# Reordering the last eight heads of the first tile in a cross-attention kernel, with eight halved slots instead of fourteen

## What is computed

```python
q = (tgt @ Wq.T).reshape(B, N, NH, dk).transpose(0, 2, 1, 3)
k = (memory @ Wk.T).reshape(B, N, NH, dk).transpose(0, 2, 1, 3)
v = (memory @ Wv.T).reshape(B, N, NH, dk).transpose(0, 2, 1, 3)
scores = jnp.einsum('bhqd,bhkd->bhqk', q, k) * scale
probs = jax.nn.softmax(scores, axis=-1)
att = jnp.einsum('bhqk,bhkd->bhqd', probs, v)
att = att.transpose(0, 2, 1, 3).reshape(B, N, D)
tgt2 = att[0]
return tgt + tgt2
```

## Time and profile before

| | before |
|---|---|
| median of 3 runs | 188.64 us (187.71 to 188.74) |
| profiled execution, its time | 188.64 us |
| its span | 186.6 us |
| busy: PE, DVE, ACT, POOL | 130.9, 102.1, 96.8, 78.1 us |
| DMA: bytes, mean rate | 71.52 MB, 383 GB/s |
| DMA packets, under 2 KB | 31424, 9008 |
| granted clock of PE, mean over the span | 0.894 |

### The profile page before, as it was taken

How to read it: one execution, slowest core, us unless ns; L and a number is a source line. 1 busy time by engine, 2 the same in 40 slices (tenths; PEclk the granted TensorE clock), 3 DMA queues, 4 the chain that set the end, 5 groups by cost and what they waited for, 6 DMA issues and landing times.

```text
span 186.6 us, 3336 instructions
## 1 busy us (share of the span) xinstructions
PE 130.9 (70%) x1224; PEld 91.9 (49%) x1224; DVE 102.1 (55%) x163; ACT 96.8 (52%) x225; POOL 78.1 (42%) x43
## 2 busy tenths in 40 slices
PE   6999999999996887998978998889885000000000
PEld 6978857677654555556756556656553000000000
DVE  0263226625527989857399659665353999900000
ACT  2344536378266979877789669798892000000000
POOL 1000000000006989800049999079992999800000
PEclk9999999999999999999999999999999755555555
DMA  6999999999999989989999999999999999999995
GB/s 218 356 357 420 407 410 412 408 409 407 411 410 384 329 297 343 341 291 319 401 386 396 393 404 407 406 404 407 411 421 413 403 416 419 407 423 421 421 420 223
DMA packets 31424, 71.52 MB, mean 383 GB/s; under 512 B 1840, under 2 KB 9008, under 8 KB 31280
## 3 DMA queue, kind: packets, MB, share of 16 engines
q1 hardware_dynamic: 31408, 71.31, 99.6%
HBM read 37.75 MB, written 33.55 MB: 382 GB/s over the span
## 4 chain that ended last, share of the span: by engine, by line
PE 54%; ACT 15%; DVE 11%; issue 6%; DVEq 1%; POOL 0%; ACTq 0%; POOLq 0%
PE bank L410 12%; PE bank L390 8%; ACT probs L609 8%; PE bank L350 8%; PE bank L368 6%; PE bank L379 6%; ACT probs_t L617 5%; PE bank L343 5%; DVE slots L743 5%; PE bank L421 4%; DVE slots L733 3%; PE bank L493 3%; DVE neg_max L689 2%; PE bank L433 1%; DVEq L67 1%
## 5 line engine op out<-in xcount | busy, mean ns | idle before, releaser
L298 POOL TENSOR_TENSOR slots<-slots,att_rows 128x512 f32<-128x512 f32 (+1 forms) x25 | 40.8, 1670 | 74.5 <-DVE att_rows L715 74.5
L609 ACT ACTIVATE probs<-bank,neg_max 128x512 f32<-128x512 f32 x64 | 44.9, 702 | 11.6 <-DVE neg_max L689 11.2
L689 DVE TENSOR_REDUCE neg_max<-bank 128x1 f32<-128x512 f32 x64 | 41.7, 682 | 13.5 <-PE bank L390 13.3
L410 PE MATMUL bank<-ident,probs 128*128 128x128 f32 x256 | 39.8, 281 | 7.7 <-ACT probs L609 6.7
L617 ACT COPY probs_t<-bank 128x512 f32<-128x512 f32 x64 | 37.7, 592 | 11.4 <-PE bank L410 10.5
L410 PEld LDWEIGHTS bank<-ident,probs 128*128 128x128 f32 x256 | 28.1, 140 | 23.4 <-ACT probs L609 17.7
L390 PE MATMUL bank<-k_t,q_t 32*128 32x512 f32 x192 | 24.2, 425 | 0.0
L307 POOL TENSOR_TENSOR slots<-slots,att_rows 128x1024 f32<-128x1024 f32 x8 | 18.6, 2382 | 5.6 <-DVE att_rows L715 5.6
L315 POOL TENSOR_TENSOR slots<-slots,att_rows 128x2048 f32<-128x2048 f32 x4 | 18.0, 4531 | 3.4 <-DVE att_rows L715 3.4
L726 DVE TENSOR_TENSOR slots<-slots,bank 128x512 f32<-128x512 f32 (+1 forms) x21 | 18.8, 907 | 0.1
L421 PE MATMUL bank<-probs_t,v 128*32 128x128 f32 x512 | 17.3, 276 | 0.7 <-ACT probs_t L617 0.7
(11 more groups left out here) (41 smaller groups left out, 91.3 us busy)
## 6 DMA issues: line engine op xcount, KB each, us to landing
slots<-in_x_dram SPq DMA_DIRECT2D x21, 1024.0 KB, 16.5
out_dram<-slots SPq DMA_DIRECT2D x28, 512.0 KB, 10.8
slots<-in_x_dram SPq DMA_DIRECT2D x22, 512.0 KB, 9.8
out_dram<-slots SPq DMA_DIRECT2D x11, 1024.0 KB, 13.5
out_dram<-slots SPq DMA_DIRECT2D x28, 256.0 KB, 3.4
ctx_raw<-in_ctx_dram SPq DMA_DIRECT2D x1, 1024.0 KB, 5.0
wq_raw<-in_L_xattn_Wq_dram SPq DMA_DIRECT2D x1, 1024.0 KB, 9.2
wv_raw<-in_L_xattn_Wv_dram SPq DMA_DIRECT2D x1, 1024.0 KB, 12.1
```

The costliest lines, as they stand in the source:

```text
L298: nc.gpsimd.tensor_tensor(xs, xs, a.unsqueeze(1).to_broadcast([P, BPS, a.shape[1]]), ALU.add).then_inc(added[g], 1)
L410: last = nc.tensor.transpose(bank[:, PT_BANK + h % 2, t * P:(t + 1) * P], probs[:, h % 2, t * P:(t + 1) * P], ident[:, :])
L609: nc.scalar.activation(probs[:, h % 2, :], bank[:, h % S_BANKS, :], ACT.Exp, bias=neg_max[:, h:h + 1], scale=1.0, accum_out=row_sum[:, h:h ...
L689: nc.vector.tensor_reduce(neg_max[:, h:h + 1], bank[:, h % S_BANKS, :], AX_X, ALU.max, negate=True).then_inc(max_ready, 1)
```

## The change

- `HALVED` shrinks from 14 groups to 8. Groups 8 to 13 are now added and stored whole with `SECOND`. POOL takes 1, 3, 5, 7 halved and 9, 11, 13, 14, 15 whole, DVE 0, 2, 4, 6 halved and 8, 10, 12 whole. The store orders follow, and `ROW_LAG` goes from 14 to 13.
- PE: the scores of heads 8 to 11 come before `turn_probs(0, 7)` and the last value chunk. `weigh_values(0, 0)` and `(0, 1)` come without query chunks between them, the scores of heads 12 to 15 right behind `turn_back`. The four query chunks of tile 1 move among heads 12 to 15, into bank 0, a bank of scores, with a wait on the exponent of head 12. The queries are turned into `PT_BANK` after `weigh_values(0, 3)`, with a wait on the copy of head 14; then come `turn_back` and the scores of tile 1, whose last pass alone waits for DVE's low part.
- After these scores PE waits for the last copy of tile 0 and does `KEEP_UP` = 4 transposes of the identity.
- The turned probabilities of heads 6 and 7 of tile 0 go into a free part of slot 13 instead of the ring, and the load of slot 13 moves to the end of the loads, behind a wait on `weigh_values(0, 1)`.
- ACT and DVE follow this order. DVE does its `FIRST` adds after the reductions of heads 12 to 15, and `empty("q_t", 1)` after `normalize(SECOND)`.

```diff
-    WARM_UP = 24
+    WARM_UP, KEEP_UP = 24, 4
...
-    HALVED = range(14)
-    POOL_HALVED, DVE_HALVED, DVE_WHOLE = (1, 3, 5, 7, 9, 11, 12, 13), (0, 2, 4, 6, 8, 10), (14, 15)
+    HALVED = range(8)
+    POOL_HALVED, DVE_HALVED = (1, 3, 5, 7), (0, 2, 4, 6)
+    POOL_WHOLE, DVE_WHOLE = (9, 11, 13, 14, 15), (8, 10, 12)
...
-    FIRST_ORDER = (0, 1, 3, 2, 5, 7, 4, 6, 9, 8, 11, 10, 12, 13)
-    SECOND_ORDER = (0, 1, 2, 3, 4, 5, 6, 7, 8, 10, 9, 11, 14, 12, 15, 13)
+    FIRST_ORDER = (1, 3, 0, 5, 2, 4, 7, 6)
+    SECOND_ORDER = (1, 3, 0, 5, 2, 7, 4, 6, 9, 8, 11, 10, 13, 14, 12, 15)
...
+        SPARE, SPARE_HEADS = 13, (6, 7)
...
-                ("v", 0, 6), ("v", 1, 7), ("v", 2, 6), ("v", 3, 7), ("q", 1, BACK_BANK), ("q_t", 1, ATT_T_BANK)]
+                ("v", 0, 6), ("v", 1, 7), ("v", 2, 6), ("v", 3, 7), ("q", 1, 0), ("q_t", 1, PT_BANK)]
...
+        def place_of_probs_t(j, h):
+
+            if j == 0 and h in SPARE_HEADS:
+                return slots[:, SPARE, 0, h % ROWS, :].rearrange("p (t n) -> p t n", n=P)
+            n = j * HEADS + h
+            return probs_t[:, (n if n < SPARE_HEADS[0] else n - len(SPARE_HEADS)) % PT_SLOTS, :, :]
...
-                if g < CTX_T:
+                if g < CTX_T and g != SPARE:
                     load(0, g)
...
             load(LAST_HALF, 1)
-
-            LAG, ROW_LAG = 4, 14
+            sp.wait_ge(att_t_summed, SPARE_HEADS[-1] // HPG + 1)
+            load(0, SPARE)
+
+            LAG, ROW_LAG = 4, 13
...
-            def scores(j, heads_at_once):
+            def scores(j, heads_at_once, low_queries_fresh=False):
                 for a, b in PASSES:
+                    if a == LO and low_queries_fresh:
+                        emptied(pe, "q_t", j)
...
             turn_probs(0, 6)
+            score_group(0, 2)
+            turn_probs(0, 7)
             value_chunk(3, 3)
-            turn_probs(0, 7)
-            score_group(0, 2)
-            query_chunk(1, 0)
+            turn_probs(0, 8)
             emptied(pe, "v", T - 1)
             weigh_values(0, 0)
-            query_chunk(1, 1)
-            turn_probs(0, 8)
-            query_chunk(1, 2)
             turn_probs(0, 9)
-            query_chunk(1, 3)
             weigh_values(0, 1)
             turn_probs(0, 10)
-            raw_queries_out(1)
             turn_back(0, range(HG // 2))
+            score_group(0, 3)
             turn_probs(0, 11)
-            score_group(0, 3)
-            turn_queries(1)
+            weigh_values(0, 2)
             turn_probs(0, 12)
             turn_probs(0, 13)
-            emptied(pe, "q_t", 1)
-            weigh_values(0, 2)
+            query_chunk(1, 0)
             turn_probs(0, 14)
+            query_chunk(1, 1)
             turn_probs(0, 15)
+            query_chunk(1, 2)
+            query_chunk(1, 3)
+            weigh_values(0, 3)
+            turn_queries(1)
+            turn_back(0, range(HG // 2, HG))
             score_group(1, 0)
-            weigh_values(0, 3)
-            turn_back(0, range(HG // 2, HG))
+
+            pe.wait_ge(probs_t_ready, HEADS)
+            for _ in range(KEEP_UP):
+                nc.tensor.transpose(bank[:, PT_BANK + 1, 0:P], ident[:, :], ident[:, :])
             heads(1)
...
             empty("v", 2)
+            head_max(0, 8)
+            head_max(0, 9)
             empty("v", 3)
-            for h in range(2 * HPG, 3 * HPG):
-                head_max(0, h)
+            head_max(0, 10)
+            head_max(0, 11)
...
             normalize(FIRST, slice(0, HEADS // 2))
-            add(FIRST, DVE_HALVED[0])
-            head_max(0, 12)
-            head_max(0, 13)
-            add(FIRST, DVE_HALVED[1])
-            head_max(0, 14)
-            empty("q_t", 1)
-            head_max(0, 15)
-            for g in DVE_HALVED[2:]:
-                add(FIRST, g)
+            for h in range(3 * HPG, HEADS):
+                head_max(0, h)
             invert_sums(0, 2)
             copy_att_t(0, 2)
+            for g in DVE_HALVED:
+                add(FIRST, g)
             invert_sums(0, 3)
+            copy_att_t(0, 3)
+            normalize(SECOND, slice(HEADS // 2, HEADS))
+            empty("q_t", 1)
             head_max(1, 0)
             head_max(1, 1)
-            copy_att_t(0, 3)
+            add(SECOND, DVE_HALVED[0])
             head_max(1, 2)
-            normalize(SECOND, slice(HEADS // 2, HEADS))
-            add(SECOND, DVE_HALVED[0])
+            add(SECOND, DVE_HALVED[1])
             head_max(1, 3)
-            add(SECOND, DVE_HALVED[1])
```

More of the change, by code:

```diff
@@ L290, in _ @@
                                     pattern=[[-1, P]], channel_multiplier=1).then_inc(ident_ready, 1)
-            for unit, groups in ((FIRST, POOL_HALVED), (SECOND, POOL_HALVED), (ROW_1, POOL_GROUPS)):
+            for unit, groups in ((FIRST, POOL_HALVED), (SECOND, POOL_HALVED + POOL_WHOLE), (ROW_1, POOL_GROUPS)):
                 pool.wait_ge(att_ready, unit)
@@ L348, in query_chunk @@
                     bank_free("q", j)
+                    if j == 1:
+                        pe.wait_ge(exp_ready, 3 * HPG + 1)
                     emptied(pe, "x0_t", j)
@@ L358, in turn_queries @@
                 raw_queries_out(j)
+                if j == 1:
+                    pe.wait_ge(probs_t_ready, HEADS - 1)
                 turn("q_t", j)
@@ L398, in score_group @@
                     pe.wait_ge(exp_ready, j * HEADS + g * HPG)
-                scores(j, range(g * HPG, (g + 1) * HPG))
+                if j == 1:
+                    pe.wait_ge(act_evacuated, sum(BY_ACT[:number["q_t", 1] + 1]))
+                scores(j, range(g * HPG, (g + 1) * HPG), low_queries_fresh=j == 1)
             def score_pair(j, pair):
@@ L421, in weigh_values @@
                         last = mm(att_t_ps[i * DK:(i + 1) * DK, g, :], v[:, t, h * DK:(h + 1) * DK],
-                                  probs_t[:, (j * HEADS + h) % PT_SLOTS, t, :], start=(t == 0), stop=(t == T - 1),
+                                  place_of_probs_t(j, h)[:, t, :], start=(t == 0), stop=(t == T - 1),
                                   tile_position=(0, i * DK))
@@ L613, in copy_transposed @@
                 act.wait_ge(transposed, j * HEADS + h + 1)
-                before = j * HEADS + h - PT_SLOTS
+                n, spare = j * HEADS + h, len(SPARE_HEADS)
+                before = n - PT_SLOTS - (spare if n < PT_SLOTS + SPARE_HEADS[-1] + 1 else 0)
                 if before >= 0:
                     act.wait_ge(att_t_summed, before // HPG + 1)
-                nc.scalar.copy(probs_t[:, (j * HEADS + h) % PT_SLOTS, :, :],
+                nc.scalar.copy(place_of_probs_t(j, h),
                                bank[:, PT_BANK + h % 2, :].rearrange("p (t n) -> p t n", t=T)).then_inc(probs_t_ready, 1)
@@ L649, in _ @@
             exponent(0, 7)
+            copy_transposed(0, 6)
             exponent(0, 8)
+            copy_transposed(0, 7)
             exponent(0, 9)
-            copy_transposed(0, 6)
-            copy_transposed(0, 7)
             exponent(0, 10)
-            empty("q", 1)
             copy_transposed(0, 8)
@@ L659, in _ @@
             copy_transposed(0, 10)
-            empty("q_t", 1)
+            copy_transposed(0, 11)
             exponent(0, 12)
-            copy_transposed(0, 11)
             exponent(0, 13)
+            exponent(0, 14)
             copy_transposed(0, 12)
-            exponent(0, 14)
+            exponent(0, 15)
             copy_transposed(0, 13)
-            exponent(0, 15)
             copy_transposed(0, 14)
             copy_transposed(0, 15)
+            empty("q", 1)
+            empty("q_t", 1)
             for j in range(1, T):
@@ L709, in normalize @@
                 if before is not None:
-                    g = (POOL_HALVED if before == SECOND else POOL_GROUPS)[-1]
+                    g = (POOL_WHOLE if before == SECOND else POOL_GROUPS)[-1]
                     dve.wait_ge(added[g], steps(before, g))
```

## The result

Against the kernel before, the changed one takes 1.0062 of its time (95% interval 1.0038 to 1.0085), which on 188.22 us is 1.2 us more. Of 20 executions of the changed kernel 14 took 193.8 to 197.0 us, at a mean granted clock of 0.85 to 0.86, which puts the median of all 20 at 194.18, 3% over the kernel before, while the ratio compares the other six (188.95 to 189.98, clock near 0.89) with the kernel before, whose 20 executions lie between 187.35 and 189.01.

What follows compares the result with a forecast made beforehand. One DMA queue, nearly always full, was taken to bound the kernel: bytes over rates plus dry time. To 188.64 us, 4.6 for rows behind the last starved store less 3.6 head start, less half of 0.94, gave +0.5: 189.1, range 187.0 to 191.2.

Steps and rivals of the forecast that it cites:

- Packets: Twelve 256 KB stores become six of 512 KB: 1.3 us less DMA work, which buys only dry time before the last starved store.
- Tile 0: Reordered heads: normalize(FIRST) at 53.9 instead of 57.26, 3.4 us sooner; normalize(SECOND) at 64.25 instead of 68.10, 3.85 sooner.
- Tile 1 unmoved: Queries turned after tile 0's last head; first reduction of tile 1 at 66.15 against 66.08 before, taken as unmoved.
- Adds and stores: SECOND's stores wait for DVE's whole adds; 10 goes out at 79.26, queue dry some 3.4 us before it; +1.0 us.
- head start: Last starved store issued at 79.26 instead of 82.86: 3.6 us, set against 4.6 us for 3.5 more rows behind it.
- The turn at 84 to 88: Stores turning to reloads ran at 306 GB/s against 400, a loss of 0.94 us; half taken as regained, leaving +0.5.
- Slot 13: Its load, moved last, may leave the queue dry up to 0.5 us, ahead of the starved store: zero cost.
- ROW_1's cover of 2.6 us: At the first ROW_1 store, landing in 5.9 against 3.3 us: stores running ahead by up to 2.6 us meet no wait.
- rival A: Faster: tile 1 sooner or its adds in gaps, SECOND's stores hardly starve; 187.3 us named, 186.0 if all came; chance 0.25.
- Rival B: Slower: granted clock falls to 1.2 GHz at the seam of tiles 0 and 1, 2.0 us on the path, 191.1; chance 0.21.

Runs made afterwards that it cites:

- the ninth run: Changed kernel with transposes of the identity in all three PE waits between tiles 0 and 1, slot 13's load moved behind the FIRST stores: 1.0091 of the kernel before.
- The seventh run: Changed kernel's new order of heads with fourteen halved slots, transposes in all three PE waits between tiles 0 and 1: 1.0037 of the kernel before.
- the second: Changed kernel with HALVED back at fourteen slots, so the reorder alone: 193.4 to 196.7 us in five of six executions, no ratio.
- fourth run: Changed kernel without the four transposes behind tile 1's scores (KEEP_UP 0): 1.0269 of the kernel before.
- the filled kernel: Changed kernel with transposes of the identity in all three PE waits between tiles 0 and 1 (5, 3 and 10): 1.0091 of the kernel before.

## Why the prediction was right, and where it was off

The forecast was 189.1 us in a range of 187.0 to 191.2, with no change of over 0.5% the likeliest case. Measured is 1.0062 of the time before, 1.2 us where the sum had 0.5, inside that step's bounds of -0.5 and 1.6, and just past the 0.5% that it called slower with a chance of 0.32. The mechanism, a queue that starves ahead of DVE's whole adds so that the packets saved buy nothing, is what the windows show. That the number held owes something to the width of the range: a later tile 1 and a credit for the turn that never came made the sum too small by 0.7 and 0.5 us, and the 14 executions of 193.8 us and more lie outside it.

- Packets. Right that they buy nothing: the windows before store 10 show dry time instead. With halved slots alone the same saving comes with 1.0124.
- Tile 0. The walk used the times of the kernel before, so the trace after has to be moved by its 1.27 us to be set against it. FIRST was walked to 53.9 and came at 52.75 + 1.27 = 54.02; SECOND was walked to 64.25 and came at 63.59 + 1.27 = 64.86. The walk was right to 0.1 for FIRST and 0.6 us too hopeful for SECOND.
- Tile 1 unmoved. 66.15 was the walk, 66.08 the kernel before, 65.63 + 1.27 = 66.90 the trace. This step failed: tile 1 comes 0.82 us later, where the walk had 0.07. The 0.6 us of SECOND are most of it, since the queries are turned behind the last head. That 65.63 looks like a confirmation is the luck of one execution's start.
- Adds and stores. 10 was to go out at 79.26 with 3.3 us to landing; it went out at 78.7, that is 79.95 lined up, with 3.9, and the dry second is at 75 to 76, before 8, as well. The head start over 82.86 is thus 2.9 us, not 3.6, which puts 0.7 us on the sum.
- The turn at 84 to 88. This term was mis-sized. The sum kept half of 0.94 us, on the ground that the new queue would not be dry there. It wasn't (share 1.00), and the low rate stayed: 266 and 328 GB/s in 83 to 88 lose 0.33 + 0.72 = 1.05 us against 400. Without that credit and with the head start of 2.9 the sum is 4.6 - 2.9 = 1.7, a little over the interval (0.7 to 1.6). Both errors went the same way, and some tenths that come back are not accounted for.
- Slot 13. Zero, and the ninth run agrees. The short dry spell that the text allowed is there (a share of 0.73 from 50 to 51; 48 to 52 ran at 339 GB/s in all, 410 before), and by the ninth run nothing ahead of the starved stores reaches the time.
- ROW_1's cover of 2.6 us. Here the text was wrong, and with it rival A's price. It took the cover from the first store alone, with tile 1 unmoved, and let 2.6 us of gain through, 186.0. The seventh run found the queue dry at 97 and had a lead of 2.8 us at the first ROW_1 landing (1.6 lined up), and ended at 1.0037. Tile 1 had come 0.99 us later, and behind the first store the rate stayed under 400 until 110, 1.06 us of it by dryness and 1.27 at a full share for a cause that no run shows. A lead at the first transfer of a stage is not yet a gain.
- Rival B, the clock, was given 0.21 and 2.0 us. The mechanism is real and frequent: it shows in the run without transposes (0.52 from 66 to 80), and the mean clock under 0.87 in 14 of 20 executions of the changed kernel, against none before, fits it. The price, 2.5 us over the kernel before in all, was too low: those 14 took 5.5 to 8.7 us more than its median, because the text let the level fall for PE's next 2.5 us of work alone, while in the profiles of the second and fourth runs it stayed low for some 14. The argument against it, that PE's waits from 60 to 72 had left the clock alone before, did not carry over to the new seam, which idles PE in another pattern. What the Trainium skill says (TensorE: Matmul & The Clock Gate, Part 1), that an idle PE goes back to half clock, agrees with the fourth run's trace as to the fall, which came in PE's wait of 1.65 us (0.83 in 66 to 67, 0.50 in 67 to 68).

What failed beyond the numbers: the forecast weighed B as one case of the sum, and not as something that a single program does in some executions and not in others.

## What to carry to other kernels

Before two profiles are compared, line them up at the last instruction that the change does not touch: here the same opening took 1.27 us more in one than in the other, enough to turn a tile that comes 0.82 us later into one that seems 0.45 sooner. When one transfer queue is full nearly throughout, look for the last moment at which it runs dry and count what is still behind it; a saving ahead of that moment buys only waiting. Before trusting a lead, follow the cover through every later stage that compute must feed. And where a reorder takes the filler work out of TensorE's waits, look at the granted clock in many executions, not in one profile.

## What the hardware showed that was not expected

- The start: the reduction of heads 4 to 7, up to which PE, ACT and DVE run the same program in all 13 profiles that were read, stands at 40.23 to 41.80 us. From there on profiles with the same order of heads, the same fillings of the seam and a clock of 1.00 agree to 0.04 us as far as ROW_1.
- The clock at the seam: PE had waits of 0.50, 0.30 and 1.65 us between 64 and 67.7, the clock fell in the last of them, and from 66 to 80 it stood at 0.52 in the mean, though PE was busy for 11.85 of these 14 us. In the kernel before, PE was busy only 2.50 of the 4 us from 60 to 64 and the clock stayed at 1.00.
- The rate where stores turn to reloads: 266 to 328 GB/s at a DMA share of 1.00, in the kernel before (306, the queue just dry) and after (266 and 328, not dry just before); with the reloads put last, 342 over the stretch of work in which the filled kernel had 291. The seventh run ran its reloads at 408 in 83 to 88, behind a dry stretch. No run shows the cause.
